# A two-layer graph network on one core: where the next chunk is loaded, and when the last pairs and carried rows are handled

## The chip, the cores and the metric

The kernel runs on one core of a Trainium2 chip, in one launch. The metric is the device time of that launch in microseconds (us), the median of several runs. The profile comes from one more execution, taken by the hardware profiler; its times are quoted on a clock of their own that starts with the span.

## The reference

Nodes: 6250 with 256 features. Edges: 206,250, sorted by destination (100,000 drawn pairs in both directions, and a loop for each node). The network runs once, then a mixture-of-experts layer:

```
def _gcn_layer(x, W, b, src, dst, norm, n_nodes):
    xt = x @ W
    msg = xt[src] * norm[:, None]
    agg = jax.ops.segment_sum(msg, dst, num_segments=n_nodes)
    return jax.nn.relu(agg + b)
norm = edge_weight * jax.lax.rsqrt(deg_out[src] * deg_in[dst] + EPS)
h6 = _gcn_layer(h5_all, W6, b6, src, dst, norm, N_NODES)
h7 = _gcn_layer(h6, W7, b7, src, dst, norm, N_NODES)
out = h7 @ Wp + bp
...
x = x + gnn(layernorm(x));  x = x + experts(layernorm(x))   # 8 experts, top 2 of a router, gelu, widths 256-512-256
```

## The kernel before, in words

**Two ways to sum over edges.** A layer multiplies a table of node rows by a weighted adjacency matrix. The matrix is cut in two parts. One part is *dense*: TensorE multiplies 128x128 tiles of edge weights by rows that have been laid into "chunks" of 30 or 31 tiles (one chunk has 18). The other part is *gathered*: GpSimd fetches the source rows of 8 tiles of edges (a "group", 128 rows to a tile) by 8 indirect DMAs from the node table, and TensorE sums each tile into its destination rows by a one-hot matrix (`sums`, L2111). A sum that runs over the end of a group or of a chunk is carried on: its last row is stored to a scratch tensor `zsum`, read back as one row into `zs` (for a group, `carry row`, L731) or into the chunk (`carry chunk`, L761), and added by `combine` (L2124). The code calls the one-row reads and the stores of the full 128 rows `store_group` (L731 or L740, in turn), `store_rows` (L752) and `carry_chunk`.

**Layer 1** runs 24 chunks and 110 groups. Its first 96 groups lie in a loop, and its chunks of edge weights are built on chip and stored for layer 2 (`chunks`, 3,283 KB each). The last 14 groups, 96 to 109, are *turns* k = 0 to 13 written out one by one. In a turn stand a group's sums, its combine, and some *pairs*. A pair is 256 finished node rows: they are read from `zsum` (`load_pair`, L776), scaled on VectorE (L1362), transposed (`pair_T`, L2133), passed through relu (`pair_relu`, L1805, ScalarE), multiplied by the weights (`project`, L2150), copied out (`pair_out`, L1814) and stored to the table that layer 2 gathers from (`store_table`, L798 or L794). Layer 2's first gather waits for the whole table. There are 25 pairs, 0 to 24. `TAIL_PAIRS` says which pairs lie in which turn.

**Layer 2** walks 113 *slots*. A slot takes at most one gather group (104 of them) and a part of a chunk: 26 chunks of 3 or 4 slots (3 for the first 8), so that chunks begin at slots 0, 3, ..., 21, 24, 28, 32, ..., 92. Each chunk is loaded from `chunks` by one DMA that SyncE issues (`load_chunk`, L770), one chunk ahead. A pair of layer 2 starts at a slot of its own and then goes through six *stages*, s0 to s5, one in each of the next slots: s0 is load, scaling, `pair_T`, `project` (L2150); s1 adds the network's result to the node row and normalizes (VectorE L1374 to L1119); s2 and s3 do the transposes of the normalized rows (L2163), the router (L2173) and the ranks within the experts' lists (L2181 to L2187), and s3 stores the pair's two results (`store_x`, `store_acc`, L815 and L819); s4 and s5 fill the experts' lists (L2212, whose input is the `one_hots` of VectorE, L1457 to L1460). The start of a pair is set by when its rows are complete. Eleven pairs ("dense") wait on chunks, the others on groups, through `groups_for`:

```
def groups_for(L, b):
    return min(2 * ceil_div(tiles_before((b + 1) * PT * P) + 2 * TG - G0[L] * TG, 2 * TG), GROUPS[L])
```

In a slot each engine works through its own list of instructions in the order written. SyncE issues all DMAs named above but the first two chunk loads; TensorE's order in a slot is the group's sums, then chunk tiles with the combine and the stages of the pairs placed between them. GpSimd gathers up to four groups ahead of the sums (a ring of 4 buffers).

**After the slots** 105 *blocks* of experts run: GpSimd takes rows of a block (L990), TensorE multiplies them (L2297, L2306) by weights that VectorE copies into place (L1582), and GpSimd adds the result to `acc` (L1003).

## Time and profile before

| | us |
|---|---|
| median of 3 runs | 3162.39 (3161.69 to 3169.01) |
| the profiled execution's own time | 3166.45 |
| its span | 3164.5 |
| TensorE busy | 2631.7 (83%) |
| GpSimd busy | 1963.4 (62%) |
| VectorE busy | 1911.0 (60%) |
| ScalarE busy | 861.5 (27%) |
| mean granted TensorE clock | 0.919 of full speed |

The profile's own time is 4.06 us above the median and 1.95 us above its span. Layer 1's last gather begins at 1519.04 us, layer 2's first at 1555.26, layer 2's last at 2638.91; the blocks of experts take the rest.

### The profile page before, as it was taken

How to read it: one execution, taken by the hardware profiler on the slowest of the kernel's cores; microseconds unless marked ns; L12 is line 12 of the kernel's file. 1: busy time of each engine (PE TensorE's matmuls, PEld its weight loads, DVE VectorE, ACT ScalarE, POOL GpSimd, SP SyncE). 2: the span in 40 equal slices, each digit the busy share in tenths (PEclk: the TensorE clock that was granted, in tenths of full speed). 3: DMA queues.
4: the chain of work that ended last, by engine and by line, in shares of the span. 5: the costliest groups of instructions: out<-in, count | busy, mean ns of one | idle time of the engine just before them, and what ended most of it. 6: DMA issues, size and time to landing. Idle time of an engine off the chain costs nothing. (4 is left out here: it accounts for less than half of the span.)

```text
span 3164.5 us, 53882 instructions
## 1 busy us (share of the span) xinstructions
PE 2631.7 (83%) x16919; PEld 2013.0 (64%) x16919; DVE 1911.0 (60%) x6028; ACT 861.5 (27%) x2052; POOL 1963.4 (62%) x1932
## 2 busy tenths in 40 slices
PE   4567479999999999995589988888888875899995
PEld 3456247676667776663466766666666553889984
DVE  9999878888888887864203545455545446522210
ACT  5677611122121222112201100000011001456652
POOL 0000277777777777777477777777777763467763
PEclk8699789999999999997899999899999885999997
DMA  4001355566665655668666766666666663344444
GB/s 129 0 22 43 115 166 181 201 204 203 199 203 193 195 188 191 203 199 276 207 201 226 259 213 213 194 217 215 226 220 221 219 226 93 60 66 71 70 67 115
DMA packets 197506, 530.79 MB, mean 168 GB/s; under 512 B 39338, under 2 KB 129247, under 8 KB 190463
## 3 DMA queue, kind: packets, MB, share of 16 engines
q0 software_dynamic: 102336, 252.47, 30.5%
q1 hardware_dynamic: 92174, 256.65, 22.4%
q10 hardware_dynamic: 2736, 18.48, 1.5%
q8 instruction: 131, 2.15, 0.3%
q14 instruction: 129, 1.05, 0.1%
HBM read 377.61 MB, written 156.24 MB: 169 GB/s over the span
## 5 line engine op out<-in xcount | busy, mean ns | idle before, releaser
L977 POOL DMA_INDIRECT arena<-table,src_i x1712 | 1673.7, 978 | 596.2 <-issue 514.5
L2098 PE MATMUL bank<-arena 128*128 128x257 f32 x4900 | 1246.5, 391 | 3.1 <-ACT zcd L1784 2.4
L2098 PEld LDWEIGHTS bank<-arena 128*128 128x128 f32 x4900 | 901.7, 194 | 202.5 <-issue 83.4
L2083 PE MATMUL bank<-arena 128*128 128x294 bf16 x2352 | 426.2, 295 | 49.6 <-DVE arena L1295 32.3
L1323 DVE TENSOR_TENSOR arena<-arena,bank 128x294 f32 x784 | 357.3, 456 | 176.4 <-PE bank L2083 164.9
L1295 DVE SCALAR_TENSOR_TENSOR arena<-iota_f,arena 128x256 f32<-128x256 f32 x784 | 366.8, 468 | 0.0
L2083 PEld LDWEIGHTS bank<-arena 128*128 128x128 bf16 x2352 | 226.4, 100 | 207.9 <-DVE arena L1323 46.3
L2111 PE MATMUL bank<-arena,s_all 128*32 128x257 f32 x3424 | 246.2, 408 | 75.1 <-DMA arena<-table,src_i 68.4
L1771 ACT COPY arena<-zero 128x2144 f32<-128x2144 f32 (+1 forms) x104 | 156.3, 1533 | 398.3 <-DMA chunks<-arena 335.9
L1003 POOL DMA_INDIRECT acc<-arena x105 | 178.7, 1702 | 126.6 <-ACT arena L1897 97.6
L1294 DVE TENSOR_SCALAR arena<-iota_key,arena 128x294 bf16<-128x294 bf16 x784 | 242.7, 310 | 0.0
L2055 PE MATMUL bank<-arena 128*128 128x150 bf16 x1616 | 152.6, 256 | 107.6 <-DVE arena L1143 72.2
L1582 DVE COPY arena<-arena 128x1024 f32 x105 | 76.2, 733 | 261.9 <-PE bank L2297 245.7
L968 POOL PARTITION_ALL_REDUCE bad_all<-bad_f x1 | 0.4, 380 | 358.4 <-DVE bad_f L1285 358.4
L2055 PEld LDWEIGHTS bank<-arena 128*128 128x128 bf16 x1616 | 132.7, 109 | 128.9 <-DVE arena L1143 107.3
L2297 PE MATMUL bank<-arena 128*128 128x128 f32 x1680 | 211.0, 280 | 0.0
L2306 PE MATMUL bank<-arena 128*128 x840 | 203.1, 384 | 8.8 <-ACT arena L1897 8.8
L2111 PEld LDWEIGHTS bank<-arena,s_all 128*32 128x32 f32 x3424 | 93.5, 114 | 178.6 <-DMA arena<-table,src_i 76.1
L1760 ACT COPY zs<-bank 127x257 f32<-127x257 f32 x107 | 40.1, 375 | 608.2 <-PE bank L2111 607.3
L2297 PEld LDWEIGHTS bank<-arena 128*128 128x128 f32 x1680 | 202.2, 197 | 0.1
L2306 PEld LDWEIGHTS bank<-arena 128*128 128x128 f32 x840 | 153.3, 193 | 28.3 <-issue 10.5
L990 POOL DMA_INDIRECT arena<-rows_x,arena x105 | 109.2, 1040 | 85.1 <-DVE arena L1487 34.0
(238 smaller groups left out, 2678.3 us busy)
## 6 DMA issues: line engine op xcount, KB each, us to landing
chunks<-arena SPq DMA_DIRECT2D x25, 3283.0 KB, 12.7
arena<-chunks SPq DMA_DIRECT2D x24, 3283.0 KB
arena<-table,src_i POOLq DMA_INDIRECT x1712
zsum<-zc SPq DMA_DIRECT2D x107, 128.5 KB, 3.2
zrow<-zsum SPq DMA_DIRECT2D x50, 257.0 KB, 4.7
arena<-in_W ACTq DMA_DIRECT2D x16, 512.0 KB, 16.9
rows_x<-arena SPq DMA_DIRECT2D x25, 264.0 KB
arena<-chunks ACTq DMA_DIRECT2D x2, 3283.0 KB
```

The costliest lines, as they stand in the source:

```text
L977: pool.indirect_dma_start(gat[:, r, j, 0:D], None, table[L], bass.IndirectOffsetOnAxis(ap=src_i[:, col:col + 1], axis=0)).then_inc(gathere ...
L1003: pool.indirect_dma_start(acc, bass.IndirectOffsetOnAxis(ap=row_e[:, j:j + 1], axis=0), ye[:, j % 2], None, compute_op=ALU.add).then_inc(y ...
L1294: dve.tensor_scalar(ohk[:, r], iota_key[:, 0:KEYS], key[:, t:t + 1], None, ALU.is_equal)
L1295: dve.scalar_tensor_tensor(out=words[:, r], in0=bc_mid(iota_f[:, :], 2), scalar=lo_f[:, t:t + 1], in1=bc_in(w_words[:, t], P), op0=ALU.is_ ...
L1323: dve.tensor_tensor(win, win, ps_b[t % len(ps_b)].rearrange("p (h w) -> p h w", w=TW), ALU.add).then_inc(added, 1)
L1771: done = act.copy(adj[:, c % 2, first:first + whole], zero[:, :].unsqueeze(2).broadcast_to([P, whole, AWID]))
L2055: last = pe.matmul(ps_do, oh_lo[:, r, j // TI, :, j % TI], whi[:, r, j // TI, :, :, j % TI].rearrange("p i n -> p (i n)"), start=False, st ...
L2083: last = pe.matmul(ps_b[t % len(ps_b)], halves[:, t % OH_RING, word, :, half], ohk[:, t % OH_RING], start=(i == 0), stop=(i == 2))
L2098: last = pe.matmul(ps_ap, adj[:, c % 2, h, 0:P], xp[:, h], start=(h == 0), stop=(h == XB_ALL - 1))
L2111: last = pe.matmul(ps_seg[q * WIN:(q + 1) * WIN, :], s_mat[:, r, q * HQ + j], gat[:, r, q * HQ + j], start=(j == 0 and not second), stop=( ...
L2297: last = pe.matmul(ps_h[j % 2][:, c], w1_e[:, j % W1_RING, k, c * P:(c + 1) * P], xeT[:, j % 2, k], start=(k == 0), stop=(k == KD - 1))
L2306: last = pe.matmul(ps_y, hs[:, j % 2, c], w2_of(e, c), start=(c == 0), stop=(c == HC - 1))
```

## The change

Three things are edited.

1. **The last turns of layer 1.** TensorE's `combine` and ScalarE's `copy_rows` of a turn stand behind the first pair of the turn, where they stood behind all of its pairs. SyncE stores or carries the group accordingly. Pair 23 moves from behind the last group into turn 12, so that one pair (24) stands behind it.
2. **The slack in `groups_for`.** It is `TG` (8 tiles), not `2 * TG`. Layer 1 needs this for pair 23 in turn 12. The function is shared: in layer 2, pairs 14, 15, 16, 17 start at slots 28, 36, 44, 52 (before: 30, 38, 46, 54), and pairs 23, 24 at 102, 105 (before: 104, 107). Layer 2 has 111 slots. The other pairs' starts are the same.
3. **Layer 2's chunk load.** It is issued behind the slot's carried rows, not right behind the store of the last chunk's rows.

```
-TAIL_PAIRS = [range(0)] * TAIL_FROM + [... for k in range(TURNS)] + [range(0)] * 2
+TAIL_PAIRS = [range(0)] * TAIL_FROM + [... for k in range(TURNS)] + [range(LATE_PAIR, NPAIR - 1), range(0)]
...
 def groups_for(L, b):
-    return min(2 * ceil_div(tiles_before((b + 1) * PT * P) + 2 * TG - G0[L] * TG, 2 * TG), GROUPS[L])
+    return min(2 * ceil_div(tiles_before((b + 1) * PT * P) + TG - G0[L] * TG, 2 * TG), GROUPS[L])
...
 # SyncE, layer 1, turn k
+                    if k == TAIL - 1:
+                        store_table(LATE_PAIR)
+                    if k % 2 == 0:
+                        store_group(0, LOOP_GROUPS + k)
                     for b in TAIL_PAIRS[k]:
+                        if b == LATE_PAIR:
+                            load_early(b)
                         if b + 2 < LATE_PAIR:
                             load_early(b + 2)
                         if b > EARLY_PAIRS:
                             store_table(b - 1)
-                    store_group(0, LOOP_GROUPS + k)
-                for b in range(LATE_PAIR, NPAIR):
-                    load_early(b)
-                for b in range(LATE_PAIR - 1, NPAIR):
-                    store_table(b)
+                        if k % 2 and b == TAIL_PAIRS[k][0]:
+                            store_group(0, LOOP_GROUPS + k)
+                    if k % 2 and not TAIL_PAIRS[k]:
+                        store_group(0, LOOP_GROUPS + k)
+                load_early(NPAIR - 1)
+                store_table(NPAIR - 1)
...
 # SyncE, layer 2, a slot
                     if c and j == 0:
                         store_rows(1, c - 1)
-                        if c + 1 < ALL:
-                            load_chunk(c + 1)
                         carry_chunk(1, c)
                     if g is not None:
                         store_group(1, g)
+                    if c and j == 0 and c + 1 < ALL:
+                        load_chunk(c + 1)
...
 # TensorE, layer 1, turn k
+                    if k == TAIL - 1:
+                        project(LATE_PAIR, 0, w7, ps_f(LATE_PAIR))
                     sums(0, n)
...
-                    for b in TAIL_PAIRS[k]:
+                    for b in TAIL_PAIRS[k][:1]:
                         tail_pair(b)
                     combine(0, n)
-                for b in range(LATE_PAIR, NPAIR):
-                    tail_pair(b)
+                    for b in TAIL_PAIRS[k][1:]:
+                        tail_pair(b)
+                pair_T(0, NPAIR - 1, (NPAIR - 1) % 2)
                 project(NPAIR - 1, 0, w7, ps_f(NPAIR - 1))
```

ScalarE's and VectorE's lists follow in the same way (`copy_rows` behind the first pair; `pair_out(23)` at the head of turn 13).

**SyncE at slot 36, where chunk 11 begins (pair 3 is then in s3).** Before: the store of the last chunk's rows (`zcd`), the chunk load, the carried rows (first into the chunk, then into `zs`), and pair 3's results to `rows_x` and `acc`. `TENSOR_LOAD` reads a register; `ISA` rows are waits.

```order
L752 DMA zsum<-zcd 128x257
L770 DMA arena<-chunks 128x6566
L744 TENSOR_LOAD bc_i
L744 ISA x2
L761 ISA
L761 DMA arena<-zsum 1x257
L725 TENSOR_LOAD bg_i
L725 ISA x2
L731 ISA
L731 DMA zs<-zsum 1x257
L815 DMA rows_x<-arena 128x2x264
L819 DMA acc<-arena 128x2x256
```

Now, at the same slot (the lines are numbered 2 higher):

```order
L754 DMA zsum<-zcd 128x257
L746 TENSOR_LOAD bc_i
L746 ISA x2
L763 ISA
L763 DMA arena<-zsum 1x257
L727 TENSOR_LOAD bg_i
L727 ISA x2
L733 ISA
L733 DMA zs<-zsum 1x257
L772 DMA arena<-chunks 128x6566
L817 DMA rows_x<-arena 128x2x264
L821 DMA acc<-arena 128x2x256
```

The chunk load moved behind two one-row reads, each of which has waits ahead of it. It still stands ahead of the two stores, and now directly so.

**The same stretch of SyncE, for pair 15.** Before, its load (`zrow`, with `in_x` behind it) comes after the stores of pair 3, at slot 38:

```order
L819 DMA acc<-arena 128x2x256
L725 TENSOR_LOAD bg_i
L725 ISA x2
L740 ISA
L740 DMA zsum<-zc 128x257
L776 DMA zrow<-zsum 128x2x257
L809 DMA arena<-in_x 128x2x256
```

Now it comes ahead of the chunk's store of rows, at the head of slot 36:

```order
L742 DMA zsum<-zc 128x257
L778 DMA zrow<-zsum 128x2x257
L811 DMA arena<-in_x 128x2x256
L746 TENSOR_LOAD bc_i
L746 ISA x2
L754 ISA
L754 DMA zsum<-zcd 128x257
```

So pair 15's s0 lies in the slot of pair 3's s3, and its s1 in the slot behind. Pairs 14, 16 and 17 moved by the same two slots; pairs 16 and 17 meet pairs 4 and 5 in this way at slots 44 and 52.

**SyncE at the end of layer 1's turns.** Before: the store of group 107's rows, the row that is carried from it, the store of group 109's rows, and then pairs 23 and 24 loaded together:

```order
L740 DMA zsum<-zc 128x257
L725 TENSOR_LOAD bg_i
L725 ISA x2
L731 ISA
L731 DMA zs<-zsum 1x257
L725 TENSOR_LOAD bg_i
L725 ISA x2
L740 ISA
L740 DMA zsum<-zc 128x257
L776 DMA zrow<-zsum 128x2x257 x2
L798 DMA table<-arena 128x2x256 x2
L794 DMA table<-arena 128x256
```

Now:

```order
L733 DMA zs<-zsum 1x257
L778 DMA zrow<-zsum 128x2x257
L800 DMA table<-arena 128x2x256 x2
L727 TENSOR_LOAD bg_i
L727 ISA x2
L742 ISA
L742 DMA zsum<-zc 128x257
L778 DMA zrow<-zsum 128x2x257
L796 DMA table<-arena 128x256
```

Pair 23's load moved ahead of the last store of `zc`; two table stores follow it there, and only pair 24's load and its table store stand behind.

**VectorE at the first block of experts.** Before, the weight copies (L1582) stand behind one result's first output (L1491) and two sets of one-hots:

```order
L1491 TENSOR_TENSOR arena<-arena,bank 128x512
L1457 TENSOR_SCALAR off_i<-iota_col,arena 128x400
L1458 TENSOR_SCALAR off_i<-iota_b,arena 128x128
L1460 TENSOR_SCALAR off_i<-iota_b,arena 128x128
L1457 TENSOR_SCALAR off_i<-iota_col,arena 128x400
L1458 TENSOR_SCALAR off_i<-iota_b,arena 128x128
L1460 TENSOR_SCALAR off_i<-iota_b,arena 128x128
L651 TENSOR_LOAD arena
L1582 ISA
L1582 COPY arena<-arena 128x1024
```

Now pair 23's scaling (L1371) and its s1 (from L1383 on) stand ahead of them (the lines are numbered 9 higher), as here, where s1 begins:

```order
L1371 TENSOR_SCALAR zr_all<-zrow,mv 128x256 x2
L1466 TENSOR_SCALAR off_i<-iota_col,arena 128x400
L1467 TENSOR_SCALAR off_i<-iota_b,arena 128x128
L1469 TENSOR_SCALAR off_i<-iota_b,arena 128x128
L1466 TENSOR_SCALAR off_i<-iota_col,arena 128x400
L1467 TENSOR_SCALAR off_i<-iota_b,arena 128x128
L1469 TENSOR_SCALAR off_i<-iota_b,arena 128x128
L1383 TENSOR_TENSOR arena<-bank,arena 128x512
L1385 TENSOR_TENSOR arena<-arena 128x512
L1119 BN_STATS st<-arena 128x6 x2
```

and here, 38 rows further on, where it ends and the copies begin:

```order
L1112 TENSOR_TENSOR rv<-rv 128x2
L1128 TENSOR_SCALAR arena<-arena,mv,rv 128x256 x2
L653 TENSOR_LOAD arena
L1591 ISA
L1591 COPY arena<-arena 128x1024
```

TensorE's list has changed beside it: the `pair_T` of pair 23, which stood between the work of the first two blocks, stands now with its `project` ahead of the first block.

## Rows read from the trace of the kernel before

In a timeline the columns are start and duration in us, engine, line, operation, output<-input, shapes, count, and in brackets the idle time before it with what ended it.

**Rows 1.** Page: busy us, share of the span, instructions.

```profile
PE 2631.7 (83%) x16919; PEld 2013.0 (64%) x16919; DVE 1911.0 (60%) x6028; ACT 861.5 (27%) x2052; POOL 1963.4 (62%) x1932
```

**Rows 2.** Waits of POOL, 1550 to 2700: us in total, times, longest.

```profile
POOL arena L977 <- PE bank L2111: 41.6, 17, 12.2
POOL arena L977 <- DMA table<-arena: 35.3, 1, 35.3
POOL arena L990 <- DVE arena L1487: 33.1, 2, 32.8
```

**Rows 3.** Waits of PE in layer 2, 1556 to 2640.

```profile
PE bank L2124 <- DMA zs<-zsum: 38.2, 17, 5.1
PE bank L2133 <- DVE zr_all L1362: 26.0, 14, 7.3
...
PE bank L2212 <- DVE off_i L1460: 22.2, 8, 11.4
```

**Rows 4.** Timeline of SP around chunk 10's start.

```profile
1918.73 0.43 SPq L770 DMA_DIRECT2D arena<-chunks  x1
1921.98 0.32 SPq L761 DMA_DIRECT2D arena<-zsum  x1
1923.29 0.30 SPq L731 DMA_DIRECT2D zs<-zsum  x1
1923.69 0.42 SPq L776 DMA_DIRECT2D zrow<-zsum  x1
```

**Rows 5.** Tile zrow, 1556 to 2640: time to landing of its loads.

```profile
DMA to landing us min/median/max: 3.0/10.9/12.0
```

**Rows 6.** Timeline of PE in chunk 10: combine and pair_T.

```profile
1931.79 0.67 PE L2124 MATMUL bank<-zs,arena 128*128 128x257 f32 x2 [1.05 <-DMA zs<-zsum]
...
1938.03 1.12 PE L2133 MATMUL bank<-ident,zr_all 128*128 128x128 f32 x4 [1.47 <-DVE zr_all L1362]
```

**Rows 7.** Timeline of SP around chunk 24's start.

```profile
2497.56 0.42 SPq L770 DMA_DIRECT2D arena<-chunks  x1
...
2504.42 0.46 SPq L819 DMA_DIRECT2D acc<-arena  x1
```

**Rows 8.** Timeline of DVE behind it.

```profile
2514.74 0.69 DVE L1374 TENSOR_TENSOR arena<-bank,arena 128x512 f32<-128x512 f32 x1 [8.39 <-DMA acc<-arena]
...
2528.44 0.36 DVE L1460 TENSOR_SCALAR off_i<-iota_b,arena 128x128 bf16<-128x128 bf16 x1
```

**Rows 9.** Timeline of PE behind it.

```profile
2528.95 1.49 PE L2212 MATMUL bank<-off_i 128*128 128x400 bf16 x4 [3.61 <-DVE off_i L1460]
```

**Rows 10.** Windows (chunks 11, 24): length; busy PE, PEld, DVE, ACT, POOL; PEclk; DMA.

```profile
1964.47:2002.81 38.34, 34.06 (x198) 25.35 (x198) 17.79 (x73) 3.08 (x8) 29.07 (x31) 0.96 0.72 232
2496.87:2546.03 49.16, 42.20 (x221) 30.15 (x221) 25.95 (x118) 4.66 (x12) 37.28 (x40) 0.83 0.63 208
```

**Rows 11.** Timeline of PE at layer 1's end.

```profile
1528.08 0.60 PE L2124 MATMUL bank<-zs,arena 128*128 128x257 f32 x2
...
1535.41 1.20 PE L2124 MATMUL bank<-zs,arena 128*128 128x257 f32 x2 [4.86 <-DMA zs<-zsum]
...
1543.87 1.12 PE L2133 MATMUL bank<-ident,zr_all 128*128 128x128 f32 x4 [4.50 <-DVE zr_all L1362]
```

**Rows 12.** Timeline of SP there.

```profile
1531.25 0.36 SPq L740 DMA_DIRECT2D zsum<-zc  x1
1534.04 0.30 SPq L731 DMA_DIRECT2D zs<-zsum  x1
...
1539.59 0.90 SPq L776 DMA_DIRECT2D zrow<-zsum  x2
...
1553.21 0.35 SPq L794 DMA_DIRECT2D table<-arena  x1
```

**Rows 13.** Timeline of DVE at the first block of experts.

```profile
2679.85 2.49 DVE L1582 COPY arena<-arena 128x1024 f32 x4
```

**Rows 14.** Timeline of PE there.

```profile
2683.44 3.62 PE L2297 MATMUL bank<-arena 128*128 128x128 f32 x16
```

More of the change, by code:

```diff
@@ L540, in slice_bounds @@
             return first_of_step(ZERO_BEHIND[i - 1] + 1) if i else 0, first_of_step(ZERO_BEHIND[i] + 1)
-        LATE_PAIR = LOOP_PAIRS + 1
-        TURNS = TAIL - TAIL_FROM - 2
-        TAIL_PAIR_COUNT = LATE_PAIR - EARLY_PAIRS
-        TAIL_PAIRS = [range(0)] * TAIL_FROM + [range(EARLY_PAIRS + TAIL_PAIR_COUNT * k // TURNS,
-                                                     EARLY_PAIRS + TAIL_PAIR_COUNT * (k + 1) // TURNS)
-                                               for k in range(TURNS)] + [range(0)] * 2
         LAST_STEPS = [STEPS * k // TAIL_FROM for k in range(TAIL_FROM + 1)] + [STEPS] * (TAIL - TAIL_FROM)
@@ L602, in groups_for @@
         def groups_for(L, b):
-            return min(2 * ceil_div(tiles_before((b + 1) * PT * P) + 2 * TG - G0[L] * TG, 2 * TG), GROUPS[L])
+            return min(2 * ceil_div(tiles_before((b + 1) * PT * P) + TG - G0[L] * TG, 2 * TG), GROUPS[L])
+        LATE_PAIR = LOOP_PAIRS + 1
+        TURNS = TAIL - TAIL_FROM - 2
+        TAIL_PAIR_COUNT = LATE_PAIR - EARLY_PAIRS
+        TAIL_PAIRS = [range(0)] * TAIL_FROM + [range(EARLY_PAIRS + TAIL_PAIR_COUNT * k // TURNS,
+                                                     EARLY_PAIRS + TAIL_PAIR_COUNT * (k + 1) // TURNS)
+                                               for k in range(TURNS)] + [range(LATE_PAIR, NPAIR - 1), range(0)]
+        assert LATE_PAIR == NPAIR - 2 and groups_for(0, LATE_PAIR) == GROUPS[0] - 2
         PAIR_IN_CHUNK = {chunks_for(b) + 1: b for b in range(EARLY_PAIRS)}
@@ L1689, in _ @@
                         tail_pair(b)
-                for b in range(LATE_PAIR, NPAIR):
-                    tail_pair(b)
+                tail_pair(NPAIR - 1)
                 next_matrix(1, 0)
@@ L1815, in pair_out, with tail_pairs @@
                 last.then_inc(p_out, 1)
-            def tail_pairs(pairs):
+            def tail_pairs(pairs, n):
                 for b in pairs[:1]:
@@ L1825, in tail_pairs @@
                         pair_out(b - 1)
+                    if b == pairs[0]:
+                        copy_rows(0, n)
+                if not pairs:
+                    copy_rows(0, n)
             def features_T(i):
@@ L1989, in _ @@
                     n = LOOP_GROUPS + k
+                    if k == TAIL - 1:
+                        pair_out(LATE_PAIR)
                     copy_sums(0, n)
@@ L2002, in _ @@
                         load_chunk(0)
-                    tail_pairs(TAIL_PAIRS[k])
-                    copy_rows(0, n)
-                tail_pairs(range(LATE_PAIR, NPAIR))
+                    tail_pairs(TAIL_PAIRS[k], n)
+                pair_root(NPAIR - 1)
+                pair_relu(0, NPAIR - 1, b6c)
                 pair_out(NPAIR - 1)
@@ L2361, in _ @@
                     n = LOOP_GROUPS + k
+                    if k == TAIL - 1:
+                        project(LATE_PAIR, 0, w7, ps_f(LATE_PAIR))
                     sums(0, n)
@@ L2368, in _ @@
                             apply_step(0, CHUNKS - 1, step)
-                    for b in TAIL_PAIRS[k]:
+                    for b in TAIL_PAIRS[k][:1]:
                         tail_pair(b)
                     combine(0, n)
-                for b in range(LATE_PAIR, NPAIR):
-                    tail_pair(b)
+                    for b in TAIL_PAIRS[k][1:]:
+                        tail_pair(b)
+                pair_T(0, NPAIR - 1, (NPAIR - 1) % 2)
                 project(NPAIR - 1, 0, w7, ps_f(NPAIR - 1))
```

## Prediction

> **What bounds the kernel now.** I read the page first: TensorE is busy for 83% of the span, GpSimd for 62% [rows 1]. Neither is full, so what counts is which wait ends last in each stage. GpSimd's own waits tell the stages. Between the layers it stands still for 35.3 us until the last rows of the table are stored; in layer 2 it waits 41.6 us in 17 pieces for TensorE's sums, that is for a gather buffer; and 32.8 us for VectorE before the first block of experts [rows 2]. A gatherer that waits for its consumer is ahead of it. So in layer 2 TensorE's list sets the pace, and TensorE's waits there are the next view: 38.2 us for carried rows (L2124), 26.0 us for a pair's scaled rows (L2133), 22.2 us for one-hots (L2212) [rows 3]. Each stall of TensorE here is paid in full, unless a later wait on its list would have been as long without it.
>
> The profiled execution took 3166.45 us, 4.06 above the median. The sum below is made against the 3166.45.
>
> **The chunk load behind the carried rows.** At chunk 10 SyncE issues the load at 1918.73, the row carried into the chunk at 1921.98, that into `zs` at 1923.29, and the dense pair's `zrow` at 1923.69 [rows 4]. All four are on one queue. The row into `zs` is 1 KB, and yet TensorE's combine still waited for it at 1931.79; `pair_T` waited for `zrow` until 1938.03 [rows 6]. Loads of `zrow` take 3.0 us at best and 12.0 at worst [rows 5]: the slow ones are those with a chunk load in front. The edit does two things.
> - Carried rows no longer stand behind 3,283 KB. Of the 38.2 us in rows 3, I put 27.4 (ten waits of 1.2 to 5.1) into slots without a dense pair. They go: −27.4. The others (about 10) end before a longer wait for `zrow`, and are worth nothing.
> - `zrow` stays behind the chunk load, which itself is issued later, by up to 1923.29 − 1918.73 = 4.6 us [rows 4]. It is issued 5.0 us behind the load, and with 10.9 (the median) to 12.0 us to landing [rows 5] it lands 15.9 to 17.0 us after the load was issued; I take 16.5, and 0.8 for the scaling. So `pair_T` follows the load by 17.3 us at least, where chunk 10 shows 1938.03 − 1918.73 = 19.3 [rows 4, 6]: of the 4.6 us, 2.6 are left at slot 33. Over the seven dense pairs at slots 33 to 85 I get 2.4 to 4.6 each, sum 22.9. At slots 10, 13 and 16 the same working gives 11.2 in all (at 16 the load waits besides for an odd slot's store), and at slot 89, where the `acc` store is the one behind the load, 5.7. Together +39.8.
>
> Net **+12.4**. Bounds: −27.4, if the late load delays nobody, and +39.8, if the rows were hidden anyway.
>
> **The shift of pairs 14 to 17.** This is the largest term and the diff names it nowhere: `groups_for` serves layer 2 too. Pairs 15, 16, 17 now start where a chunk starts and where dense pairs 3, 4, 5 are in s3. Before, one chunk has this form, chunk 24 (pair 21 starts in pair 9's s3), and it is my template. Its load is issued at 2497.56, pair 9's `acc` store at 2504.42 [rows 7]. VectorE stood 8.39 us until that store landed, at 2514.7, 17.1 us after the load; then it worked through pair 21's s1, 14 us, before the next one-hots were ready at 2528.8 [rows 8], for which TensorE waited until 2528.95 [rows 9]. Chunk 24 took 49.16 us, with 42.20 of TensorE busy; chunk 11, without an s1 behind a late store, 38.34 with 34.06 [rows 10].
>
> For chunk 11 in the new order: load at the start +7.2 (the carried rows' time, as chunk 24's 2504.42 − 2497.56 = 6.9), store landed 17.1 behind that, at +24.3, one-hots ready 14.1 later, TensorE goes on at +38.4. The work behind that point took 2546.03 − 2528.95 = 17.1 us in chunk 24, partly at the lower clock (0.83 against 0.96 granted over the two chunks [rows 10]); I take 15.7. So chunk 11 lasts 54.1 instead of 38.3: **+15.8**. Chunks 13 and 15 have the same form: +16 each. The stages s2 and s3 (about 5 us of TensorE, the greater part of the 8.1 us by which the two busy times of rows 10 differ) come out of chunks 12, 14, 16, but there `pair_T` of the dense pair waits for a `zrow` behind the load, and TensorE would only wait there longer: 0. Pair 14 moves to slot 28 alone: its 5 us of work come into chunk 9, whose wait for carried rows of 5.1 was already given back above: 0. Total **+48**. From below: TensorE's wait is then 10 us a chunk, and if the moved work is given back, 3 × 10 = +30; if the store lands as in the old order, 17 us after the chunk's start, 3 × 3 = +9 (TensorE's wait of 3.61 [rows 9] three times is 11). From above: 3 × 17.7 = +53.
>
> Here the Trainium skill can be weighed ("DMA: Bandwidth & Descriptors", "Queues, rings and completion order", and "Two DMAs through the same engine are not ordered" in the same page). It says that one queue of one DMA engine starts descriptors in the order written, and that nothing orders them across the 16 engines. By the first, a store issued behind the load lands behind it, as rows 7 and 8 show (17.1 us); by the second, a store could slip past where an engine has little of the chunk, and the sum would come out at 3166.45 + 12.4 + 9 − 3.3 + 10.5 − 4.06 = 3191. The trace has no such case.
>
> **The last turns of layer 1.** The chain before: combine(107) at 1528.08, the store of its rows at 1531.25, the carried row at 1534.04, combine(109) at 1535.41 after a wait of 4.86, then the store and the load of pairs 23 and 24 together, at 1539.59, `pair_T` at 1543.87, the table's last store at 1553.21 [rows 11, 12]; layer 2's first gather follows 2 us behind. Now combine(107) stands behind the first pair of its turn, not the second: some 5.6 us earlier, at about 1522.5. But pair 23's chain (load 2.9, scaling, `pair_T`, relu, `project`: 1539.59 to 1549.1 before) goes in between the carried row and combine(109), and SyncE's store of pair 23's table rows stands ahead of the store of group 109's. From combine(107) to the first gather I count 29.5 us: 1552 against 1555.3. **−3.3**. Bounds: 0 (the second `zrow` and its chain run one after the other, they ran together), −15 (everything of pair 23 is hidden).
>
> **The end of layer 2.** Two slots fewer, but the gathers end at 2640 in any case, and the last sums after them. Pair 23's s1 now stands on VectorE ahead of the first blocks' weight copies (2679.85 [rows 13]). An s1 is 11.5 us of VectorE's chain (2514.74 to the one-hots [rows 8], less those), and starts behind `project(23)`. The first block's product, 2683.44 before [rows 14], comes at 2696.8: +13.4. TensorE's 2.9 us for pair 23 then lie ahead of the blocks, not between them: **+10.5**. It is paid, since the blocks are TensorE's and follow without large gaps. Bounds: +4 (gathered block rows hide more) and +14.
>
> **Sum.** +12.4 + 48 − 3.3 + 10.5 = +67.6; 3166.45 + 67.6 = 3234.1, and 4.06 less for the median: **3230**.
>
> **Rivals.**
> - *It gets faster, by the carried rows.* One mechanism: what sits behind the chunk load isn't late, because the 16 engines take it beside the load. Then −27.4 stands alone in layer 2: 3162.4 − 27.4 − 3.3 + 10.5 = 3142. It decides if a `zrow` behind a load lands within 8 us. For it: the row into `zs` behind the same load was there 8.5 us after its issue [rows 4, 6]. Against: 12.0 in rows 5. Chance 0.12.
> - *The order costs as computed, the shift little* (+9): 3162.4 + 12.4 + 9 − 3.3 + 10.5 = 3191; without any cost of the shift 3182. For it: one template only. Chance 0.2.
> - *Gains and losses cancel:* the carried rows' 27.4 us pay for about half of a late `zrow` each and for a cheap shift: within 3153 to 3172. Chance 0.05.
> - The forecast, 3205 to 3255: 0.63.
>
> **Numbers.** A measurement of this kernel can tell about 0.3%, 9.5 us. Faster holds the first rival, 0.12; same 0.05; slower 0.83. The range from 3168 to 3258 leaves out the first rival and part of the third below, and little above.
>
> **What the profile after would show.** Right: TensorE's waits at L2124 (now L2138) for `zs` down from 38 to about 10 us; at L2133's line up from 26 to over 45; at L2212's line up from 22 to over 45, in slots 37, 45, 53, 8 to 13 us each, with VectorE waiting for `acc<-arena` just before; GpSimd's waits for TensorE's sums up by some 40. First gather of layer 2 at 1552, first block product 11 to 14 us later than its layer's end asks. Wrong, if `acc` lands less than 12 us after the chunk load; if chunks 12, 14, 16 get shorter by 5 us each; or if TensorE's lost time is found before a gather instead.

## The result: slower by 3.1%, more than forecast

| | us |
|---|---|
| changed kernel, median of 4 runs | 3267.43 (3264.18 to 3271.42) |
| kernel before, on the same chip | 3165.7 (3161.69 to 3172.0) |
| ratio | 1.0314, 95% interval 1.029 to 1.0339: 92 to 107 us more |
| predicted | 3230 (range 3168 to 3258) |

The profiled execution of the changed kernel took 3271.42 us. The direction was right, the size was not: 67.6 us were forecast, 99 measured (the ratio times 3165.7; the two medians alone differ by 102). In this section lines of the changed kernel are named by its own numbers: L2147 is `pair_T`, L2138 the combine, L2226 the lists of experts, L772 the chunk load.

The waits of TensorE in layer 2, 1556 to 2740 here (us in total, times, longest), which answer to [rows 3]:

```profile
PE bank L2147 <- DVE zr_all L1371: 105.0, 20, 11.9
PE bank L2226 <- DVE off_i L1469: 60.6, 6, 13.4
PE bank L2125 <- DMA arena<-table,src_i: 26.2, 4, 16.4
```

The waits for carried rows are gone, all 38.2 us of them (there is no row of L2138 <- DMA any more). The waits for a pair's scaled rows have risen from 26.0 to 105.0, those for one-hots from 22.2 to 60.6. GpSimd shows the same time from its side, waits for a free buffer up from 41.6 [rows 2] to 130.7:

```profile
POOL arena L986 <- PE bank L2125: 130.7, 21, 13.6
POOL arena L986 <- DMA table<-arena: 38.0, 1, 38.0
```

**Chunk 10, as [rows 4 to 6].** SyncE's timeline, the loads' time to landing, TensorE's `pair_T`:

```profile
1942.06 0.30 SPq L733 DMA_DIRECT2D zs<-zsum  x1
1942.40 0.38 SPq L772 DMA_DIRECT2D arena<-chunks  x1
1942.88 0.41 SPq L778 DMA_DIRECT2D zrow<-zsum  x1
```

```profile
DMA to landing us min/median/max: 2.9/14.3/15.8
```

```profile
1958.01 1.11 PE L2147 MATMUL bank<-ident,zr_all 128*128 128x128 f32 x4 [9.01 <-DVE zr_all L1371]
```

The chunk began at 1935.74. The load goes out 6.7 us later, `zrow` right behind it, and TensorE now waits 9.01 us. The median load of a pair's rows takes 14.3 us to landing, where it took 10.9 [rows 5].

**Chunk 11, which answers to chunk 24 in [rows 7 to 10].** SyncE, VectorE, TensorE, and the window of the whole chunk:

```profile
1990.05 0.38 SPq L772 DMA_DIRECT2D arena<-chunks  x1
...
1991.01 0.47 SPq L821 DMA_DIRECT2D acc<-arena  x1
```

```profile
2007.88 0.69 DVE L1383 TENSOR_TENSOR arena<-bank,arena 128x512 f32<-128x512 f32 x1 [16.09 <-DMA acc<-arena]
...
2021.54 0.31 DVE L1469 TENSOR_SCALAR off_i<-iota_b,arena 128x128 bf16<-128x128 bf16 x1
```

```profile
2022.00 1.49 PE L2226 MATMUL bank<-off_i 128*128 128x400 bf16 x4 [12.38 <-DVE off_i L1469]
```

```profile
1982.30:2039.50 57.20, 41.47 (x220) 29.99 (x220) 25.48 (x118) 4.65 (x12) 34.68 (x37) 0.79 0.53 174
2288.90:2329.80 40.90, 35.70 (x198) 25.91 (x198) 18.68 (x77) 3.07 (x8) 30.80 (x33) 0.87 0.69 224
```

The store to `acc` lands 17.8 us after the load's issue and 25.6 after the chunk's start; TensorE goes on 39.7 after it. The prediction had 17.1, 24.3 and 38.4. The chunk takes 57.2 us, 54.1 were forecast. The second window is chunk 17, of which the prediction said nothing: 40.9 us, against 36.2 before.

**Chunk 17** has a *group pair*, one that waits on groups and not on chunks (18, started at slot 62), and TensorE waits for no one-hots in it. SyncE's timeline and TensorE's `pair_T`:

```profile
2293.55 0.38 SPq L772 DMA_DIRECT2D arena<-chunks  x1
...
2299.68 0.37 SPq L742 DMA_DIRECT2D zsum<-zc  x1
2310.25 0.38 SPq L778 DMA_DIRECT2D zrow<-zsum  x1
```

```profile
2314.63 1.11 PE L2147 MATMUL bank<-ident,zr_all 128*128 128x128 f32 x4 [4.28 <-DVE zr_all L1371]
```

The odd group's store (L742; only groups with an odd number store their rows, the even ones read the carried row) was issued at 2299.68, behind the load; the pair's rows may only be read when it has landed, and SyncE issues that read (L778) at 2310.25. TensorE waits 4.28 us, where before it waited nothing at this place. This is the step that the prediction lacks.

**The ends of the two layers.** Layer 2's first gather begins at 1563.05, where it was 1555.26 and 1552 was forecast. Of these 7.8 us, 5.0 were there before: layer 1's last gather began at 1524.08 and not at 1519.04. Experiment 3 times the tail alone. At the first block of experts, VectorE's s1 of pair 23 and its weight copies, and TensorE's first product:

```profile
2780.68 0.69 DVE L1383 TENSOR_TENSOR arena<-bank,arena 128x512 f32<-128x512 f32 x1 [4.16 <-PE bank L2164]
...
2792.44 2.50 DVE L1591 COPY arena<-arena 128x1024 f32 x4 [0.48 <-issue]
```

```profile
2793.19 3.79 PE L2311 MATMUL bank<-arena 128*128 128x128 f32 x16 [8.03 <-DVE arena L1591]
```

The copies stand 11.8 us behind the s1's start, as forecast (11.5), and TensorE waits 8.03 us for them.

### The profile page after: what moved, and what is told of

The parts are those of the page before. It is cut to its first block and busy times, and to the rows that moved or that the text cites. A ratio compares the mean times of both kernels' runs of the same rounds, so it can differ in the third digit from the quotient of the medians.

```text
span 3269.4 us, 53876 instructions
## 1 busy us (share of the span) xinstructions
PE 2640.7 (81%) x16919; PEld 2014.3 (62%) x16919; DVE 1912.0 (58%) x6030; ACT 861.2 (26%) x2052; POOL 1958.8 (60%) x1932
## 5 line engine op out<-in xcount | busy, mean ns | idle before, releaser
L2125 PE MATMUL bank<-arena,s_all 128*32 128x257 f32 x3424 | 256.5, 421 | 77.8 <-DMA arena<-table,src_i 73.4
L1012 POOL DMA_INDIRECT acc<-arena x105 | 171.4, 1633 | 145.3 <-ACT arena L1909 116.0
L999 POOL DMA_INDIRECT arena<-rows_x,arena x105 | 107.2, 1021 | 84.2 <-DVE arena L1496 34.1
## 6 DMA issues: line engine op xcount, KB each, us to landing
zsum<-zc SPq DMA_DIRECT2D x107, 128.5 KB, 3.3
```

The source lines that it names most:

```text
L1012: pool.indirect_dma_start(acc, bass.IndirectOffsetOnAxis(ap=row_e[:, j:j + 1], axis=0), ye[:, j % 2], None, compute_op=ALU.add).then_inc(y ...
L2125: last = pe.matmul(ps_seg[q * WIN:(q + 1) * WIN, :], s_mat[:, r, q * HQ + j], gat[:, r, q * HQ + j], start=(j == 0 and not second), stop=( ...
```

## The experiments

They were made in three sets after the result: 1 to 4, 5 to 8, 9 to 12. "Before" is the kernel before on the same chip as each set, with medians of 3174.4, 3161.0 and 3162.73 us. A difference in us is the recorded ratio times that median. The two medians' own difference lies within some 4 us of it, but for experiments 2 (28, not 36) and 6 (87, not 75). Theory A is mine: *whatever is behind a chunk load lands with it*, so each small transfer that TensorE's list needs soon is late if the load was issued ahead of it, and moving the load only chooses which ones. Its first form said that the saved waits for carried rows come back as longer waits for pairs' rows.

**1. The load order alone.** In the kernel before:

```
                         store_rows(1, c - 1)
-                        if c + 1 < ALL:
-                            load_chunk(c + 1)
                         carry_chunk(1, c)
                     if g is not None:
                         store_group(1, g)
+                    if c and j == 0 and c + 1 < ALL:
+                        load_chunk(c + 1)
```

> The kernel before with one edit: in layer 2, SyncE issues the chunk load behind the slot's carried rows. Theory A (the waits for carried rows that go away come back in full as longer waits for the pairs' rows, because those rows are read behind a later load): slower by 25 to 45 us, the waits for zs near 0, the waits of the pairs' transposes for scaled rows up from 26 to some 80 us. Theory B (the term of the prediction stands, saved waits are kept): slower by about 12 us. Theory C (the carried rows' gain stands alone): faster by 20 to 27 us.

Measured: 3218.05 us against 3174.4, ratio 1.0146 (1.0121 to 1.0171), +46 us (38 to 54). The prediction's +12.4 is excluded, and so is a gain; theory A's 25 to 45 fits at its upper end. TensorE's waits in layer 2 (1565 to 2699, from its first gather to its last), and chunk 13 on SyncE and TensorE:

```profile
PE bank L2133 <- DVE zr_all L1362: 112.5, 21, 11.3
...
PE bank L2212 <- DVE off_i L1460: 23.8, 5, 11.4
```

```profile
2081.31 0.38 SPq L770 DMA_DIRECT2D arena<-chunks  x1
...
2085.12 0.37 SPq L740 DMA_DIRECT2D zsum<-zc  x1
2097.57 0.38 SPq L776 DMA_DIRECT2D zrow<-zsum  x1
```

```profile
2102.06 1.12 PE L2133 MATMUL bank<-ident,zr_all 128*128 128x128 f32 x4 [6.27 <-DVE zr_all L1362]
```

```profile
2074.30:2116.70 42.40, 35.19 (x197) 25.71 (x197) 18.29 (x76) 3.07 (x8) 29.24 (x31) 0.88 0.65 210
2102.06:2109.45 7.39, 6.46 (x28) 3.81 (x28) 2.21 (x6) 0.84 (x2) 2.85 (x3) 0.52 0.26 73
2109.45:2116.70 7.25, 7.25 (x48) 5.64 (x44) 6.28 (x30) 1.12 (x3) 5.34 (x6) 1.00 0.37 96
```

In the kernel before, this chunk took 36.5 us, with a wait of 1.9 for the carried row, the load issued at its very start, the odd group's store landed 18 us into it, and no wait at `pair_T`. Now the 1.9 are gone, and 6.27 are waited at `pair_T`, 27.8 us into the chunk where it was 24.8. The chunk takes 42.4, 5.9 more. The other 2.9 us lie right behind the wait. There the granted clock is 0.52 of full speed for 7.4 us, and 1.00 again after them (the last two windows), where the kernel before had 1.00 in that place. `pair_T`, `project` and the sums take 1.12, 3.78 and 1.71 us, before 0.60, 2.00 and 1.08. So a chunk pays more than its late transfer.

In the seven chunks 9, 11, ..., 21 TensorE now waits 4.6 to 7.8 us at the group pair's `pair_T`, 41.3 in all, and waited nothing there before; the waits for carried rows that went away in the same chunks were 20.7.

**2. The earlier pairs alone.** `groups_for` with 8 tiles of slack for layer 2, 16 for layer 1, in the kernel before.

```
-... + 2 * TG - G0[L] * TG, 2 * TG), GROUPS[L])
+... + (1 if L else 2) * TG - G0[L] * TG, 2 * TG), GROUPS[L])
```

> The kernel before with one edit: the slack in groups_for is 8 tiles for layer 2 alone, so pairs 14 to 17 and 23, 24 start earlier; the chunk load stays in front of the carried rows. Theory A (the shift is costly because an acc store behind a chunk load holds up the next pair's s1): the store lands 17 us after the load, which is issued at the chunk's start, 7 us earlier than in the changed kernel, so chunks 11, 13, 15 get 8 to 10 us longer each, about +25 to +30, and +9 at the first blocks for pair 23: +35 to +40 in all. Theory B (the shift is costly only together with the late load): under +15 in all. Theory C (the shift carries the whole excess of the result): over +60.

Measured: 3202.4, ratio 1.0115 (1.0075 to 1.0156), +36 (24 to 49), as A said. The place is the expected one. VectorE and TensorE in chunk 11, which began at 1957.58 with the load at 1958.92:

```profile
1977.57 0.69 DVE L1374 TENSOR_TENSOR arena<-bank,arena 128x512 f32<-128x512 f32 x1 [10.54 <-DMA acc<-arena]
```

```profile
1991.95 1.49 PE L2212 MATMUL bank<-off_i 128*128 128x400 bf16 x4 [7.05 <-DVE off_i L1460]
```

The store landed 18.7 us after the load, and TensorE waited 7.05. The chunk took 51.3 instead of 38.3. But chunk 12 took 43.4 instead of 48.5: with the load at a chunk's start, the work that was moved out of a chunk is given back (chunks 14 and 16 gave 2.4 and 2.5 us).

**3. Layer 1's tail alone.** The changed kernel with layer 2's slack as before; the call of `load_chunk` goes back to its old place too.

```
-... + TG - G0[L] * TG, 2 * TG), GROUPS[L])
+... + (2 if L else 1) * TG - G0[L] * TG, 2 * TG), GROUPS[L])
```

> The kernel before with the edit of layer 1's last turns alone; layer 2 is as before (its slack and its load order too). The profile of the changed kernel has 35 us from the combine of group 107 to layer 2's first gather where the kernel before has 27. Theory A (the tail costs, because pair 23's chain stands between the last carried row and the last combine): slower by 2 to 6 us. Theory B (the term of the prediction): faster by 3 us. Theory C (what the profile shows later is only the slower gathers ahead of the turns): within 1 us.

Measured: 3171.77 against 3174.4, ratio 0.9995 (0.9978 to 1.0012). That is −7 to +4 us: no difference that can be told, and no verdict between the theories but that none of them is large. The 7.8 us that the changed kernel's profile shows at layer 2's first gather are no measure by themselves: GpSimd's wait between the layers was 27.9 us in experiment 2 and 41.3 in experiment 1, which have the old tail both. But over all profiles the first gather begins at 1549.9 to 1565.8 in the ten with the old tail (mean 1556.6) and at 1563.1 to 1565.1 in the four with the new one (mean 1564.2). So a loss of a few us is likelier than the gain that was forecast.

**4. The changed kernel without the earlier pairs.** The same edit of `groups_for` as in 3, with the new load order.

> The changed kernel with layer 2's slack of 16 tiles back, so that the pairs start where they did before; the tail of layer 1 and the order of the load are the changed ones. Theory A (order some +35, tail some +4, and the two parts add): 3195 to 3215 us. Theory B (order +12): 3175 to 3185. If the shift carries the excess: under 3175.

Measured: 3229.86, ratio 1.0181 (1.0154 to 1.0208), +57; above what A said. By experiments 1 and 3 it should be +46 and 0; the intervals of 1 and 4 overlap, and nothing in layer 2's text differs. By the profiles the rest lies within chunks 0 to 24 (1034.8 against 1022.7 us, in the table below), not in the tail; why stays open. Between two profiles a chunk that no edit touches can differ by some 4 us.

Here are the chunks' lengths, from first tile to first tile, in us; chunks 11, 13, 15 and 17 have a group pair, 10 to 16 (even) a dense one:

| chunk | before | 1: order | 4: order and tail | 2: earlier pairs | changed |
|---|---|---|---|---|---|
| 9 | 37.7 | 37.8 | 37.5 | 35.5 | 34.5 |
| 10 | 45.8 | 48.0 | 47.3 | 42.3 | 46.6 |
| 11 | 38.3 | 42.7 | 41.6 | 51.3 | 57.2 |
| 12 | 48.5 | 46.9 | 48.0 | 43.4 | 45.9 |
| 13 | 36.5 | 42.4 | 41.0 | 49.2 | 54.0 |
| 14 | 45.2 | 46.3 | 47.5 | 42.8 | 46.6 |
| 15 | 38.5 | 42.0 | 43.1 | 49.1 | 55.7 |
| 16 | 45.9 | 46.3 | 47.2 | 43.4 | 47.0 |
| 17 | 36.2 | 42.4 | 42.7 | 38.1 | 40.9 |
| 0 to 24 | 973.9 | 1022.7 | 1034.8 | 1001.2 | 1061.6 |

**5. The load at the head of the next slot,** in the kernel before: behind a dense pair's read, ahead of the odd group's store.

```
-                        if c + 1 < ALL:
-                            load_chunk(c + 1)
                         carry_chunk(1, c)
+                    if c and j == 1 and c + 1 < ALL:
+                        load_chunk(c + 1)
                     if g is not None:
                         store_group(1, g)
```

> The kernel before, with layer 2's chunk load issued at the head of a chunk's second slot, behind the row read of a dense pair but ahead of the odd group's store. Theory A (what is read or stored behind a chunk load lands with it): dense pairs' rows land about 3 us after their issue, not 11, and no longer hold up TensorE; but the odd group's store is still behind the load, now a later one, so the group pairs, which wait for that store, come later than before by 5 to 8 us in chunks 9, 11, ..., 21. The waits of L2133 move from chunks 10, 12, ... to chunks 11, 13, ...; time within 15 us of before either way. Theory B (a late load is bad whatever stands behind it): slower by more than the 46 us of the first experiment.

Measured: 3166.47, ratio 1.001 (0.9987 to 1.0033): no difference that can be told. A later load is not bad by itself (theory B is out), and the waits moved as A said: chunks 10, 12, 14 took 43.7, 44.9 and 43.3 us (45.8, 48.5, 45.2 before), chunks 11, 13, 17 took 42.0, 43.4 and 41.8 (38.3, 36.5, 36.2).

**6. The load on ScalarE's queue,** issued behind its copy of the last chunk's rows.

```
 # ScalarE, slot j == 0 of chunk c
                     copy_chunk(1, c - 1)
+                    if c + 1 < ALL:
+                        load_next(c + 1)
 # SyncE
-                        if c + 1 < ALL:
-                            load_chunk(c + 1)
```

> The kernel before, with layer 2's chunk loads issued by ScalarE on its own queue, right behind its copy of the last chunk's rows, that is at the same moment of the chunk as before. Theory A (order within the one queue of SyncE is what delays the small transfers): carried rows, pairs' rows and acc stores land in 3 to 5 us, TensorE's waits for zs fall under 10 us and those at L2133 under 15; faster by 30 to 60 us. Theory B (the 3283 KB fill the DMA engines whichever queue they come from): waits and time as before, within 5 us.

Measured: 3248.14, ratio 1.0237 (1.0192 to 1.0281): 75 us slower, which neither theory had. Chunk 13 on ScalarE's queue, on SyncE's, and at TensorE's combine:

```profile
2089.10 0.34 ACTq L1912 DMA_DIRECT2D arena<-chunks  x1
```

```profile
2089.65 0.36 SPq L752 DMA_DIRECT2D zsum<-zcd  x1
2104.28 0.32 SPq L761 DMA_DIRECT2D arena<-zsum  x1
```

```profile
2107.00 1.20 PE L2128 MATMUL bank<-zs,arena 128*128 128x257 f32 x2 [5.89 <-DMA zs<-zsum]
```

```profile
SPq L744 <- DMA zsum<-zcd: 293.6, 24, 13.8
```

The load left ScalarE at 2089.10, before the store of the last chunk's rows left SyncE at 2089.65. That store of 128.5 KB landed 14.6 us later, though its own queue was otherwise empty: the packets of the store ahead of it were all under way by 2089.1. In the kernel before it is ahead of the load and lands in 3.3. SyncE waits for it 12 us in each of the 24 chunks (2.7 before), and everything behind waits too. The DMA view of 2094 to 2100 shows the two queues side by side (packets, MB, share of the 16 engines' time; q10 is ScalarE's, q1 SyncE's):

```profile
q10 hardware_dynamic: 84, 2.21, 85.8%
q1 hardware_dynamic: 77, 0.08, 3.8%
```

Both queues moved about as many packets, but in the trace's packet records one of the load has 26,264 bytes and takes about 0.98 us, one of the store 1,028 bytes and 0.05 us. So the store got about one small packet through for each big one. Its 128 packets over 16 engines are eight each, by my estimate some 8 us of waiting for big ones; the first of them moved 5.1 us after the issue. My theory was too narrow in naming SyncE's queue. Theory B named the engines rightly, but expected the old waits. Whether the store would have landed early with the load issued just after it on the other queue was not tested.

**7. The load in a chunk's third slot** (second in chunks of three), behind the pair's read and the carried row.

```
+                    if c and c + 1 < ALL and j == (2 if SPANS[c] == 4 else 1):
+                        load_chunk(c + 1)     # behind store_group; the old call is taken out
```

> The kernel before, with layer 2's chunk load issued in a chunk's third slot (second in chunks of 3), behind the slot's pair rows and its carried row. Theory A: nothing that TensorE waits for within the chunk is behind the load any more; waits for zs and at L2133 nearly gone, the load (about 15 us) still lands before the next chunk starts or a few us late; faster by 20 to 60 us. Theory B (a late load is bad by itself): TensorE then waits for the chunk's data at the start of each chunk, 5 us or more in each, and the kernel is slower than before.

Measured: 3148.94 against 3161.0, ratio 0.9949 (0.9927 to 0.9972), 16 us faster, less than A's 20 to 60; theory B is out. Chunks 10 to 21 took 476 us in all, before 502; but chunk 5 took 52.4 (37.7) and chunk 6 took 43.5 (34.1): in chunks of three slots an `acc` store came to stand behind the load. VectorE's wait there, in chunk 5:

```profile
1739.52 0.69 DVE L1374 TENSOR_TENSOR arena<-bank,arena 128x512 f32<-128x512 f32 x1 [18.52 <-DMA acc<-arena]
```

**8. The load behind the carried rows only in chunks without a group pair;** 4, 6 and the odd ones from 9 to 21 keep the old order (`GROUP_PAIR_IN(c)` is true where a group pair starts in a later slot of the chunk than its first).

```
-                        if c + 1 < ALL:
+                        if c + 1 < ALL and GROUP_PAIR_IN(c):
                             load_chunk(c + 1)
                         carry_chunk(1, c)
                     if g is not None:
                         store_group(1, g)
+                    if c and j == 0 and c + 1 < ALL and not GROUP_PAIR_IN(c):
+                        load_chunk(c + 1)
```

> The kernel before, with the load behind the carried rows in those chunks alone in which no group pair starts (9 chunks, 4, 6, 9, 11, ..., 21, keep the old order). Theory A (the cost of the order is made of two parts, dense pairs' rows behind a later load, and group pairs' rows that wait for an odd group's store behind the later load): by the lengths of the chunks in the first experiment, +18 us of its +46. Theory B (the cost lies with the dense pairs alone, as the prediction had it): the whole +40 or more.

Measured: 3180.96, ratio 1.0054 (1.0031 to 1.0076), +17 (10 to 24), as A said. So of experiment 1's +46 some 17 lie with the other chunks, the dense pairs' above all, and some 29 (within 11 or so) with the group pairs', which the prediction left out. The profiles agree: those nine chunks are 30.4 us longer in experiment 1 than before.

**9. As 7, for chunks of four slots alone;** those of three keep the old order.

```
+                    if j == 2 and c + 1 < ALL and SPANS[c] == 4:
+                        load_chunk(c + 1)
```

> The kernel before, with the chunk load in the third slot of a chunk, behind the pair rows and the carried row, for the chunks of four slots alone; the eight chunks of three slots keep the old order. In the third-slot experiment chunks 5 and 6, of three slots, took 24 us longer than before and the rest took about 38 us less. Theory A (a transfer behind the load is late, one ahead of it isn't): those 24 us go, faster than before by 25 to 40 us, bounded by the gathers, for which TensorE then waits. Theory B (the two differences were chance): as the third-slot experiment, 0.5% faster.

Measured: 3133.71 against 3162.73, ratio 0.9915 (0.9885 to 0.9945), 27 us faster than the kernel before: the best version here. Waits of TensorE (1561 to 2615, first gather to last) and GpSimd in layer 2:

```profile
PE bank L2113 <- DMA arena<-table,src_i: 44.8, 11, 16.6
PE bank L2214 <- DVE off_i L1462: 26.7, 8, 16.0
PE bank L2135 <- DVE zr_all L1364: 19.5, 14, 1.7
```

```profile
POOL arena L979 <- PE bank L2113: 6.1, 3, 5.5
```

Carried rows cost 0.4 us, pairs' rows 19.5, and GpSimd waits 6.1 us for a buffer, not 41.6. TensorE now waits for gathers instead (44.8, before 25.0): in chunks 22 and 23 it waits 15.1 us for them, where before it waited nothing, so there the gathers have become the bound.

**10. The changed kernel with the load as in 9.**

> The changed kernel (tail of layer 1, earlier pairs, all as changed) with the chunk load placed as in the previous experiment instead of behind the carried rows. Theory A (the cost of the earlier pairs 14 to 17 is an acc store that lies behind a chunk load, so it goes when the load moves): chunks 11, 13, 15 take under 45 us where the changed kernel has 54 to 57, and only the cost of pairs 23 and 24 is left of the shift: 5 to 15 us above the previous experiment, 3140 to 3160. Theory B (the earlier start is costly by itself, by more work in a chunk where a dense pair's stages lie): 3170 to 3200.

Measured: 3146.91, ratio 0.9949 (0.9924 to 0.9973). The changed kernel loses its whole excess when only the place of the chunk load is changed. VectorE's wait for the `acc` store in chunk 11, and the chunk's window:

```profile
1975.72 0.69 DVE L1385 TENSOR_TENSOR arena<-bank,arena 128x512 f32<-128x512 f32 x1 [5.23 <-DMA acc<-arena]
```

```profile
1960.90:2005.80 44.90, 38.50 (x221) 28.49 (x221) 25.51 (x118) 4.67 (x12) 34.12 (x36) 0.92 0.69 220
```

The store, issued at 1969.51, landed in 6.2 us, where the changed kernel's took 16.9 from its own issue (17.8 from the load's); chunks 11, 13, 15 took 44.8, 40.3 and 40.1. Chunks 9 to 16 together took 308 us, in experiment 9 they took 314: no cost of the earlier pairs 14 to 17 by themselves can be seen.

**11. The last pairs alone:** the smaller slack in layer 2 for pairs 23 and 24 only (`1 if L and b > 22 else 2`), in the kernel before.

> The kernel before, with the smaller slack for pairs 23 and 24 of layer 2 alone, so that they start at slots 102 and 105 and the other pairs where they did. The prediction's term: 10 us slower, by VectorE's s1 of pair 23 ahead of the first blocks' weight copies (range 4 to 14). The rival: the two slots fewer and the earlier last pairs take as much off the end, within 3 us.

Measured: 3181.66, ratio 1.0063 (1.004 to 1.0086), +13 to +27. In the profiles the time from chunk 25's start to the end of the span is 625.7 to 631.7 us in the five kernels with the early pair 23, and 612.4 to 618.5 in those without: 13 us more. The term was right in kind; its 10.5 lie below the interval.

**12. Both edits of layer 2, without layer 1's.**

> The kernel before with both edits of layer 2, the load behind the carried rows and the smaller slack, and without the edit of layer 1. If the two edits add: before plus 46 plus 36, a ratio of 1.026. Theory A (the late load makes the shift dearer, since the acc store behind it is 7 us later in each of three chunks, about +15 to +20): a ratio of 1.030 to 1.033. If the whole result of the change (1.031) is reached without the tail, the tail is free in this order too.

Measured: 3260.8, ratio 1.0321 (1.0298 to 1.0343), +102. The whole of the change's cost (99) is there without the tail. The two edits alone cost 46 and 36; the 20 us on top are uncertain by some 17. About 10 of them can be seen: chunks 12, 14 and 16 took 45.8, 46.9 and 46.5 us here, and 43.4, 42.8 and 43.4 with the earlier pairs alone. With the late load they wait for the dense pair's rows in any case, and give back nothing of the work that was taken from them (46.9, 46.3 and 46.3 with the late load alone).

## Why the prediction was wrong

**The step that failed** is in the order's term: "Carried rows no longer stand behind 3,283 KB. [...] They go: −27.4." The waits went, the time did not. The forecast for this term was +12.4; experiment 1 measured +46 (38 to 54), at or above my upper bound of +39.8. Two things were missing. First, in chunks with a group pair the odd group's store is issued just behind the load, too, and the pair's read waits for its landing. I had followed only dense pairs, whose read stands next to the load in the list; experiment 8 puts 29 of the 46 us on the others. So in seven of the ten slots that I booked as a saving, TensorE waits in experiment 1 for the same load a slot later. Second, these waits at `pair_T` are followed by a lower granted clock (0.52 over the 7.4 us behind the 6.27 us of chunk 13; over chunks 0 to 24 0.94 before and 0.90 in experiment 1), and this term priced waits alone.

**In the changed kernel itself** the two edits of layer 2 meet: pairs 14 to 17 are read ahead of the load, so of the seven group pairs only those in chunks 17, 19 and 21 wait. By chunks, from the two profiles, in us:

| chunks | forecast | changed − before |
|---|---|---|
| 11, 13, 15: `acc` store behind the load | +48.0 − 9.0 | +53.6 |
| 17, 19, 21: group pairs | −6.6 | +14.5 |
| 9: pair 14 | −5.1 | −3.2 |
| 10 to 20 (even), 23: dense pairs | +22.9 | +7.4 |
| 3, 4, 5 (slots 10, 13, 16) | +11.2 | +12.3 |
| 24 (slot 89) | +5.7 | +5.7 |
| 2, 8, 22: carried rows alone | −6.7 | −2.7 |
| 0, 1, 6, 7 | 0 | −0.1 |
| all | +60.4 | +87.5 |

The largest miss is the 21 us of the group pairs. The second is an error of my sum: the 54.1 us of chunk 11 were set against 38.3 with its wait for the carried row in it, and the same waits of chunks 11, 13 and 15 (3.35, 1.88 and 3.80 in the profile before) stood in the −27.4 too. Those 9.0 us were counted twice; without that the sum is 76.6. Against these, the dense pairs were 15 us too dear: their `pair_T` came 19.5 us later in all, close to what I worked out, but 7.2 us of waits for one-hots behind it went away, which I had not set against it. That the total came as near as it did is partly luck.

**The shift of pairs 14 to 17** had the right mechanism and place, and nearly the right size: landing, one-hots and length as worked out from chunk 24 (+48 forecast, +53.6 against the kernel before; +41 against experiment 4, whose group pairs wait in these chunks already). That chunks 12, 14 and 16 give nothing back ("TensorE would only wait there longer: 0") held with the late load: they are 3.2 us shorter than in experiment 4, which is within what two profiles differ by. Over chunks 0 to 24 the shift shows +27 against experiment 4, so the chunks other than 11, 13 and 15 are 14 us shorter in all: 3.2 in 12, 14 and 16, 3.0 in chunk 9, whose pair is now read ahead of the load, and 0.7 in chunk 10, which lost pair 14's work; the rest is spread over chunks that the shift does not touch. With the load at a chunk's start the zero was false: 10 us came back (experiment 2).

**The tail** was forecast at −3.3 and measured at −1.6 (−7 to +4), so it is neither shown nor excluded. Its chain did not come out: from combine(107) to the first gather I counted 29.5 us, and the four profiles with the new tail show 35.1 to 36.2. **The last pairs:** +10.5 forecast, 13 by the profiles, 13 to 27 by the medians.

So the sum 12.4 + 48 − 3.3 + 10.5 = 67.6 stands against 46 to 57 (experiments 1, 4), 27, 0, and 13, together 86 to 97, measured 99 (92 to 107). The rival that ends on the other side, a `zrow` that lands beside the load within 8 us, was false (14.3 median). The Trainium skill's sentence that nothing orders transfers across the engines ("DMA: Bandwidth & Descriptors", "Two DMAs through the same engine are not ordered") gained nothing here: in no row did a store slip past the load, and in experiment 6 even another queue's store came 14.6 us late. The Trainium skill's other sentence there, that one queue of one engine starts descriptors in the order written, agrees with rows 7 and 8 and with the 17.8 us of chunk 11, but experiment 6 shows that the shared engines delay a small transfer without it.

Open are the 11 us between experiments 1 and 4. Wait and clock were separated for chunk 13 of experiment 1 alone (3.0 and 2.9 us), not for the whole.

## What to carry to other kernels

In this kernel a big load delayed every transfer that was issued behind it on its queue, until the load was nearly or wholly through. So when it is moved, list every small transfer on both sides, and for each who waits for its landing, two or three slots on; a wait that disappears at one of them is no gain if the next one hangs on the same load. The right place for such a load is behind the last small transfer that its own stretch needs, as long as it still lands before its use: here that was worth 27 us (experiment 9), where the change cost 99. A slack in a shared planner function moves work in every stage that calls it, and must be costed there.

## What was not expected of the hardware

A store of 128.5 KB on SyncE's queue took 14.6 us when a load of 3283 KB had been issued 0.55 us earlier on ScalarE's queue, and 3.3 us where the load was issued behind it on the same queue. A separate queue did not shield it: the engines served the two queues about packet for packet (77 against 84 in 6 us), and a packet of the load has 26,264 bytes, one of the store 1,028. And time lost in TensorE's waits drew more after it: 3.0 us of delay in chunk 13 cost 5.9, with the granted clock at 0.52 for the 7.4 us behind the wait.
